# A graph layer's gathers: three of the four groups of a tile are made to wait for TensorE's results

## The chip, the core and the metric

The kernel runs on one core of a Trainium2 chip. Its engines work side by side and wait for each other through semaphores: TensorE (PE, with its weight loads as PEld), VectorE (DVE), ScalarE (ACT), GpSimd (POOL), which here does little more than issue gathers, and SyncE (SP), which issues the plain DMAs. The metric is the time of one execution on the device in microseconds (us).

## The reference, cut to what matters

```python
h = xn @ W                                             # 6250 nodes x 256, 4 heads of 64
e = leaky_relu(a_src[src] + a_dst[dst], 0.2)           # 106250 edges, sorted by dst
ex = exp(e - segment_max(e, dst)[dst])
out = segment_sum(ex * h[src], dst) / segment_sum(ex, dst)
x = x + sigmoid(out + bias) + mix(xn)                  # mix: linear attention with a gate
x = x + ffn(layernorm(x))                              # two layers, 1024 wide; half of the nodes kept
```

The part that matters is `h[src]`: for each edge a row of 260 numbers (256 features and 4 scores) is fetched from memory by the number of its source node.

## The kernel before, in words

Edges are worked through in 52 tiles of 2048 (`NI`, `IE`), nodes in 49 tiles of 128 (`NT`). After a stage that makes the table `feat_d` there is one long block in which every engine runs the same list of parts per step k (`steps`), some parts with a lag: in step k the edges of tile k are scored, weighted and summed, node tile k-5 is merged and gated (`MERGE`), k-6 is summed and normed (`SUM`), k-7 goes through the feed-forward layers (`FF1`, `GELU`), k-8 is put out (`OUT`). Steps 0 to 4 also hold the chunks of the attention's context. Steps 10 to 49 are a loop of two steps per round; the steps around it are written out. Each engine works in the order of its own list; there is no scheduler. The last step with gathers to issue is that of tile 51, and after it some steps run without any.

The order of TensorE in a step is: `turn_scores` (L1503, signals `scores_turned`), `first_ff1` (L1573), `turn_maxima` (L1512, signals `max_turned`), `project` (L1556), `other_ff1` (L1573), `first_sums` and `other_sums` (L1545, each signals `sums_done`), `scores_ahead` (L1487), context chunks, `ff2` (L1524, signals `ff2_done`), `mixer` (L1466, then L1474, which signals `gate_done`), `turn_normed` (L1565, signals `xn2_turned`). "Signals" means that the last matmul of the part adds one to the semaphore.

Those who wait for these signals: VectorE's `outputs` (L1164) for `ff2_done`, `maxima` (L1142, L1145) for `scores_turned`, `differences` (L1154) for `max_turned`; ScalarE's `gates` (L1390, L1394) for `gate_done` and `keep_turned` (L1400) for `xn2_turned`. TensorE's `first_ff1` in turn waits for `keep_turned`. ScalarE's `hidden` (L1407) reads both halves of the first layer, `keep_one` (L1379) copies the sums out, and VectorE's L1134 ends the leaky scores that `turn_scores` turns. L1171 is the product of rows and weights, whose four parts the sums wait for.

GpSimd's `fill(k)` issues 16 gathers for tile k in 4 groups of 4 (`GI`, `TG`), each gather 128 rows, into one of two halves of `ring`. A group may be written when the sums of tile k-2 have read the half: groups 0 and 1 wait for its first sums, groups 2 and 3 for its other ones. VectorE's `scores(k)` needs all four groups, about a step after they are asked for.

Of the kernel before, what the change touches and what calls it, by code (L numbers as in the profile page):

```python
# [42 lines left out]
LAG_MERGE, LAG_SUM, LAG_FF1, LAG_OUT = 5, 6, 7, 8  # L43
# [20 lines left out]
def known_below(i, n):  # L64

    return isinstance(i, int) and i < n


def number(eng, v):

    return v if isinstance(v, int) else eng.snap(eng.to_reg(v))


def gps_layer(nc, x, src, dst, W, att_src, att_dst, gnn_bias, Wqkv, Wproj, bproj, ln_g, ln_b, Wg1, bg1, Wg2, bg2,
# [16 lines left out]
    with ExitStack() as ctx:  # L91
# [5 lines left out]
        def S(name):  # L97

            if name not in named:
                named[name] = ctx.enter_context(nc.semaphore(name))  # L100
            return named[name]
# [121 lines left out]
        with nc.Block() as block:  # L223
# [29 lines left out]
            @block.sync  # L253
            def _(sp):
                sp.dma_start(ed_i[:, 0:IE], src.rearrange("(k e) -> k e", e=IE)).then_inc(S("edges_in"), 16)
                sp.dma_start(ed_i[:, IE:2 * IE], dst.rearrange("(k e) -> k e", e=IE)).then_inc(S("edges_in"), 16)
                for o, i in wide:
                    sp.dma_start(o, i).then_inc(S("weights_in"), 16)
                with nc.allow_non_contiguous_dma(reason="small columns"):
                    for o, i in columns:  # L260
                        sp.dma_start(o, i).then_inc(S("weights_in"), 16)
                for n in range(7):
                    sp.dma_start(big[:, n * XC:(n + 1) * XC, :],
                                 x.rearrange("(t p) c -> p t c", p=P)[:, n * XC:(n + 1) * XC, :]).then_inc(S(f"x{n}_in"), 16)
                for o, i in later:
                    sp.dma_start(o, i).then_inc(S("ffn_in"), 16)

                sp.wait_ge(S("breaks_made"), 1)
                for h in range(HEADS):
                    sp.dma_start(brk_d[:, :, h, :], br_f.rearrange("k (g e) -> k g e", g=GI)).then_inc(S("lists_out"), 16)  # L270
                sp.wait_ge(S("dloc_made"), 2)
                sp.dma_start(dloc_d, dl_b).then_inc(S("lists_out"), 16)
                sp.wait_ge(S("zeroed"), 1)
                sp.dma_start(adst_d[NT * P:ROWS, :], zero[:, 0:SPLIT // 2].bitcast(BF16)).then_inc(S("zeros_out"), 16)
                sp.wait_ge(S("ffn_in"), 32)
# [372 lines left out]
        def gather(pool, u, g):  # L648

            for j in range(TG):  # L650
                q = g * TG + j
                pool.indirect_dma_start(  # L652
                    out=ring[:, u * TI + q, 0:AW], out_offset=None, in_=feat_d,
                    in_offset=bass.IndirectOffsetOnAxis(ap=idx[:, u, q:q + 1], axis=0),
                ).then_inc(S(f"rows_in{u}{g}"), 16)
# [182 lines left out]
        def steps(eng, parts_of_body):  # L838

            loop_from = LAG_OUT + 2 + (LAG_OUT % 2)

            def body(k, u):
                for lo, hi, f in parts_of_body:
                    if lo <= (k if isinstance(k, int) else loop_from) < hi:
                        f(k - lo, (u - lo) % 2)
            for k in range(loop_from):
                body(k, k % 2)
            loop_to = NI - 2 - NI % 2  # L850
            with eng.Fori(loop_from // 2, loop_to // 2) as half:
                for u in range(2):
                    body(half * 2 + u, u)
            for k in range(loop_to, NT + LAG_FF1):
                body(k, k % 2)
# [39 lines left out]
        with nc.Block() as block:  # L895
            @block.gpsimd
            def _(pool):
                def fill(k, u):
                    for g in range(GI):
                        made, used = number(pool, k + 1), None  # L900
                        if not known_below(k, 2):
                            used = number(pool, NB * (k - 2) + g // 2 + 1)
                        pool.wait_ge(S("idx_made"), 2)
                        if g == 0:
                            pool.wait_ge(S("idx_made"), made)
                        if used is not None:
                            pool.wait_ge(S("sums_done"), used)
                        gather(pool, u, g)

                steps(pool, [EDGES(fill)])  # L910
                pool.wait_ge(S("scores_done"), NI)
                pool.iota(hotT[:, 0:30].bitcast(I32), pattern=[[1, 15]], base=1, channel_multiplier=0
                          ).then_inc(S("digits_made"), 1)
# [742 lines left out]
```

## Time and profile before

| | |
|---|---|
| Time, median of 3 runs | 2197.3 us (2191.99 to 2205.76) |
| Profiled execution | 2191.5 us, its span 2189.4 us |
| Mean granted TensorE clock | 0.721 |
| Busy: PE, PEld, DVE, ACT, POOL | 53%, 42%, 49%, 26%, 38% |
| Moved by DMA | 210.63 MB, mean 96 GB/s |

No engine is busy for much more than half of the span. The page's chain of the last work covers only the end of the program, since it breaks off at the first wait whose end it can't name, so it says nothing on the middle, where the time is.

### The profile page before, as it was taken

Reading aid. Unit: us, or ns where it says so; the run is one execution under the profiler, and the core shown is the slowest. Engines: PE = TensorE matmul, PEld = TensorE weight load, DVE = VectorE, ACT = ScalarE, POOL = GpSimd, SP = SyncE. Lnnn points to the kernel's source line nnn. Section 1 sums busy time; section 2 is a strip of 40 time slices with the busy share of each in tenths; the row PEclk is TensorE's granted clock in tenths of the full one; section 3 lists DMA queues with packets and bytes.
Section 4 is the critical chain, followed back from the end, with each engine's and each line's share of the span. In section 5 each row is a group of like instructions: output and inputs, shape, how many; then the busy total and the mean of one; then the engine's idle time right before and its main releaser. Section 6 shows DMA issues by size and latency. Waiting matters only on the chain. (4 is left out here: it accounts for less than half of the span.)

```text
span 2189.4 us, 27080 instructions
## 1 busy us (share of the span) xinstructions
PE 1152.6 (53%) x6567; PEld 909.7 (42%) x6567; DVE 1077.7 (49%) x2779; ACT 564.1 (26%) x1347; POOL 827.8 (38%) x872
## 2 busy tenths in 40 slices
PE   1993455445555555454545454545454545454682
PEld 1772233334444344444444444444444444343571
DVE  8883354544444444444444444444444444353557
ACT  2442122122222222222222222222222222232360
POOL 3003435255353534343434343434343434343200
PEclk9997566767676767676767676767676767676795
DMA  8556334243232323232333233333332333333203
GB/s 238 175 189 118 103 92 125 72 114 98 75 98 75 96 76 92 80 92 80 92 80 94 78 93 79 92 80 92 80 93 79 94 78 90 82 90 82 71 22 117
DMA packets 165932, 210.63 MB, mean 96 GB/s; under 512 B 51115, under 2 KB 130539, under 8 KB 165791
## 3 DMA queue, kind: packets, MB, share of 16 engines
q0 software_dynamic: 39936, 110.81, 19.8%
q1 hardware_dynamic: 125959, 99.41, 16.1%
q8 instruction: 14, 0.23, 0.0%
q14 instruction: 23, 0.19, 0.0%
HBM read 165.80 MB, written 44.30 MB: 96 GB/s over the span
## 5 line engine op out<-in xcount | busy, mean ns | idle before, releaser
L652 POOL DMA_INDIRECT ring<-feat_d,idx x832 | 802.4, 964 | 1066.2 <-issue 556.0
L1573 PE MATMUL bank<-late,w_s 128*128 128x128 f32 x1568 | 311.3, 381 | 678.9 <-ACT late L1400 676.0
L1573 PEld LDWEIGHTS bank<-late,w_s 128*128 128x128 f32 x1568 | 303.0, 292 | 702.4 <-issue 643.3
L1164 DVE TENSOR_TENSOR big<-bank,b2row 128x256 f32 (+1 forms) x49 | 20.8, 424 | 621.3 <-remote 621.3
L1390 ACT ACTIVATE sc<-bank,hbg 128x128 f32<-128x128 f32 x98 | 30.7, 364 | 820.9 <-remote 809.7
L1171 DVE TENSOR_TENSOR ring<-ring,bank 128x1024 f32<-128x1024 f32 x208 | 240.0, 1217 | 1.8 <-ACT bank L1360 1.8
L1545 PE MATMUL bank<-ring,hot 128*64 128x265 f32 x1664 | 212.3, 407 | 38.9 <-DVE ring L1171 32.5
L1524 PE MATMUL bank<-w_s,hT 128*128 128x256 f32 x784 | 185.9, 390 | 3.7 <-ACT hT L1407 3.7
L1545 PEld LDWEIGHTS bank<-ring,hot 128*64 128x64 f32 x1664 | 121.7, 143 | 113.1 <-issue 50.8
L1524 PEld LDWEIGHTS bank<-w_s,hT 128*128 128x128 f32 x784 | 146.9, 193 | 22.7 <-ACT hT L1407 4.3
L1407 ACT ACTIVATE hT<-bank,b_s 128x128 f32<-128x128 f32 x392 | 110.6, 372 | 42.3 <-PE bank L1573 41.7
L1423 PE MATMUL bank<-big,sc 128*128 (+1 forms) x196 | 69.5, 501 | 89.3 <-ACT big L1341 53.9
L1423 PEld LDWEIGHTS bank<-big,sc 128*128 128x128 f32 x196 | 43.3, 242 | 112.2 <-issue 84.4
L1360 ACT ACTIVATE bank<-diff 128x64 f32<-128x64 f32 x52 | 11.8, 228 | 295.8 <-DVE diff L1158 283.2
L1556 PE MATMUL bank<-wproj_s,sc 128*128 128x256 f32 x196 | 86.2, 585 | 0.0
L1379 ACT ACTIVATE wout<-bank 128x265 f32<-128x265 f32 x104 | 40.9, 393 | 162.2 <-PE bank L1545 162.2
L1503 PE MATMUL bank<-ident,lk 128*16 128x128 f32 x208 | 35.3, 292 | 85.8 <-issue 61.8
L1142 DVE TENSOR_TENSOR_SCAN forth<-brk,bank 16x512 f32<-16x512 f32 x52 | 62.5, 1202 | 22.5 <-remote 14.6
L1032 DVE TENSOR_TENSOR late<-late,big 128x256 f32<-128x256 f32 x49 | 20.9, 426 | 103.7 <-ACT big L1341 53.7
L1089 DVE TENSOR_TENSOR hot<-bank,dlocT 128x512 f32<-128x512 f32 x104 | 66.5, 680 | 0.0
L1154 DVE TENSOR_TENSOR ring<-bank,lastT 128x64 f32<-128x64 f32 x52 | 11.7, 225 | 110.7 <-PE bank L1512 105.3
L1407 ACT ACT_TABLE_LOAD x49 | 62.9, 1283 | 8.7 <-PE bank L1573 7.9
(231 smaller groups left out, 1733.8 us busy)
## 6 DMA issues: line engine op xcount, KB each, us to landing
parts_d<-wout SPq DMA_DIRECT2D x208, 66.2 KB
lists<-dloc_d SPq DMA_DIRECT2D x104, 128.0 KB
ring<-feat_d,idx POOLq DMA_INDIRECT x832
parts_d<-hot SPq DMA_DIRECT2D x50, 265.0 KB, 2.9
parts<-parts_d SPq DMA_DIRECT2D x49, 265.0 KB
xs<-in_x SPq DMA_DIRECT2D x74, 128.0 KB
feat_d<-parts SPq DMA_DIRECT2D x49, 130.0 KB, 2.8
big<-in_x SPq DMA_DIRECT2D x7, 896.0 KB, 11.1
```

The lines of the kernel that those rows point to most:

```text
L652: pool.indirect_dma_start(out=ring[:, u * TI + q, 0:AW], out_offset=None, in_=feat_d, in_offset=bass.IndirectOffsetOnAxis(ap=idx[:, u, q:q ...
L1089: V.tensor_tensor(hot[:, tiles, :], iota_ps.unsqueeze(1).to_broadcast([P, 2 * TG, WIN]), dlocT[:, bass.ds(k, 1), tiles].rearrange("p a q - ...
L1142: V.tensor_tensor_scan(forth[:, :], brk[:, 0:GE], bk_t[0:TI, :], LOWEST, ALU.add, ALU.max).then_inc(S("forth_made"), 1)
L1171: V.tensor_tensor(feats, feats, ex[:, g * TG:(g + 1) * TG, :].unsqueeze(3) .to_broadcast([P, TG, HEADS, HD]), ALU.mult).then_inc(S("scaled ...
L1379: A.activation(wout[:, n, :], bank[2 + n][:, 0:SW], ACT.Copy).then_inc(S("sums_kept"), 1)
L1407: A.activation(hT[:, m, :], bank[6 + m // 4][:, (m % 4) * P:(m % 4 + 1) * P], ACT.Gelu_apprx_tanh, bias=b1_s[:, m:m + 1]).then_inc(S("gelu ...
L1423: mm = T.matmul(bk_c[t][:, 0:C], sc[:, u, t * P:(t + 1) * P], big[:, bass.ds(i, 1), :].rearrange("p a c -> p (a c)"), start=s, stop=e)
L1503: mm = T.transpose(bk_t[0:TI, :].rearrange("r (e j) -> r j e", j=TG)[:, j, :], lk[:, u, j, :], ident[:, :])
L1524: mm = T.matmul(bk_o[:, 0:C], hT[:, m, :], w2_s[:, m, :], start=(m == 0), stop=(m == FT - 1))
L1545: mm = T.matmul(bank[2 + n][c * WIN:(c + 1) * WIN, 0:SW], hot[:, q, :], ring[:, u * TI + q, 0:SW], start=(j == 0), stop=(j == TG - 1))
L1556: mm = T.matmul(bk_t[:, 0:C], sc[:, u, t * P:(t + 1) * P], wproj_s[:, t, :], start=(t == 0), stop=(t == CT - 1))
L1573: mm = T.matmul(bank[6 + m // 4][:, (m % 4) * P:(m % 4 + 1) * P], w1_s[:, t, m * P:(m + 1) * P], xn2T[:, t * P:(t + 1) * P], start=(t == 0 ...
```

## The change

Per tile k and group g of the gathers one more wait is put ahead of the group's first gather. Group 1 waits for `ff2_done` of step k-2, group 2 for `scores_turned` of step k-1, group 3 for `max_turned` of step k-1. Group 0 is as before. The waits are left out where there is nothing yet to wait for (group 1 up to tile 8, groups 2 and 3 of tile 0). No instruction moves on TensorE, VectorE, ScalarE or SyncE.

```diff
-                        made, used = number(pool, k + 1), None
+                        made, used, pace = number(pool, k + 1), None, None
                         if not known_below(k, 2):
                             used = number(pool, NB * (k - 2) + g // 2 + 1)
+                        if g == 1 and not known_below(k, LAG_FF1 + 2):
+                            pace = ("ff2_done", number(pool, k - LAG_FF1 - 1))
+                        if g >= 2 and not known_below(k, 1):
+                            pace = (("scores_turned", "max_turned")[g - 2], number(pool, k))
                         pool.wait_ge(S("idx_made"), 2)
                         if g == 0:
                             pool.wait_ge(S("idx_made"), made)
+                        if pace is not None:
+                            pool.wait_ge(S(pace[0]), pace[1])
                         if used is not None:
                             pool.wait_ge(S("sums_done"), used)
                         gather(pool, u, g)
```

GpSimd in the loop, the first of its two steps before: two rows are a group of four gathers, and L71 makes a number for a wait.

```order
150 L652 DMA ring<-feat_d,idx 128x260 [waits sums_done,idx_made]
151 L652 DMA ring<-feat_d,idx 128x260 x3
152 L652 DMA ring<-feat_d,idx 128x260 [waits sums_done,idx_made]
153 L652 DMA ring<-feat_d,idx 128x260 x3
154 L71 ISA
155 L652 DMA ring<-feat_d,idx 128x260 [waits sums_done,idx_made]
156 L652 DMA ring<-feat_d,idx 128x260 x3
157 L652 DMA ring<-feat_d,idx 128x260 [waits sums_done,idx_made]
158 L652 DMA ring<-feat_d,idx 128x260 x3
```

And the same step now:

```order
150 L652 DMA ring<-feat_d,idx 128x260 [waits sums_done,idx_made]
151 L652 DMA ring<-feat_d,idx 128x260 x3
152 L71 ISA
153 L652 DMA ring<-feat_d,idx 128x260 [waits sums_done,ff2_done,idx_made]
154 L652 DMA ring<-feat_d,idx 128x260 x3
155 L71 ISA
156 L652 DMA ring<-feat_d,idx 128x260 [waits sums_done,scores_turned,idx_made]
157 L652 DMA ring<-feat_d,idx 128x260 x3
158 L71 ISA
159 L652 DMA ring<-feat_d,idx 128x260 [waits sums_done,max_turned,idx_made]
160 L652 DMA ring<-feat_d,idx 128x260 x3
```

The gathers stand in the same order; three of the four groups have one more name in their waits, and two more numbers are made for them.

## Rows read from the trace of the kernel before

**Rows 1.** The page: busy by engine, and the costliest groups' idle time and releasers.

```profile
PE 1152.6 (53%) x6567; PEld 909.7 (42%) x6567; DVE 1077.7 (49%) x2779; ACT 564.1 (26%) x1347; POOL 827.8 (38%) x872
...
L1573 PE MATMUL bank<-late,w_s 128*128 128x128 f32 x1568 | 311.3, 381 | 678.9 <-ACT late L1400 676.0
```

**Rows 2.** Waits from 530 to 2055 us: who waited for whom, sum, times, longest.

```profile
ACT sc L1390 <- remote: 786.9, 42, 19.2
PE bank L1573 <- ACT late L1400: 657.1, 42, 16.3
...
DVE big L1164 <- remote: 608.7, 42, 15.6
```

**Rows 3.** Timeline of one loop step: start, duration, engine, line, [idle before <- releaser].

```profile
1221.58 2.01 PE L1545 MATMUL bank<-ring,hot 128*64 128x265 f32 x16 [0.66 <-DVE ring L1171]
...
1224.61 1.19 POOL L652 DMA_INDIRECT ring<-feat_d,idx  x1 [15.34 <-PE bank L1545]
...
1226.01 3.70 PE L1524 MATMUL bank<-w_s,hT 128*128 128x256 f32 x16
1226.04 0.39 ACT L1379 ACTIVATE wout<-bank 128x265 f32<-128x265 f32 x1 [1.87 <-PE bank L1545]
...
1228.70 0.94 POOL L652 DMA_INDIRECT ring<-feat_d,idx  x1 [0.31 <-issue]
...
1230.53 0.71 PE L1474 MATMUL bank<-hidT,wg_s 64*128 64x128 f32 x4
...
1233.45 0.60 PE L1503 MATMUL bank<-ident,lk 128*16 128x128 f32 x4 [1.85 <-issue]
...
1243.74 0.95 POOL L652 DMA_INDIRECT ring<-feat_d,idx  x1 [0.30 <-issue]
1247.92 0.42 DVE L1164 TENSOR_TENSOR big<-bank,b2row 128x256 f32 x1 [14.60 <-remote]
1247.95 0.63 ACT L1390 ACTIVATE sc<-bank,hbg 128x128 f32<-128x128 f32 x2 [18.39 <-remote]
...
1253.00 0.66 PE L1512 MATMUL bank<-ident,srow 16*128 16x16 f32 x4
...
1261.55 0.94 POOL L652 DMA_INDIRECT ring<-feat_d,idx  x1 [16.86 <-issue]
```

**Rows 4.** Groups by line on GpSimd, 525 to 2052 us: 42 tiles of 16.

```profile
L652 POOL DMA_INDIRECT ring<-feat_d,idx x672 | 647.2, 963 | 889.5 <-issue 500.3 <-PE bank L1545 389.2
```

**Rows 5.** Timeline: first gathers of the first and the last of these tiles.

```profile
530.75 0.95 POOL L652 DMA_INDIRECT ring<-feat_d,idx  x1 [17.16 <-PE bank L1545]
...
2030.14 1.19 POOL L652 DMA_INDIRECT ring<-feat_d,idx  x1 [15.38 <-PE bank L1545]
```

**Rows 6.** Timeline of a step without gathers.

```profile
2066.19 0.39 ACT L1379 ACTIVATE wout<-bank 128x265 f32<-128x265 f32 x1 [0.81 <-PE bank L1545]
...
2073.35 0.63 ACT L1390 ACTIVATE sc<-bank,hbg 128x128 f32<-128x128 f32 x2 [1.85 <-PE bank L1474]
...
2074.73 0.42 DVE L1164 TENSOR_TENSOR big<-bank,b2row 128x256 f32<-128x256 f32 x1
...
2084.45 0.39 ACT L1379 ACTIVATE wout<-bank 128x265 f32<-128x265 f32 x1 [0.92 <-PE bank L1545]
```

**Rows 7.** Windows: a run of gathers, the 3 us after it, the rest, a step without.

```profile
1225.00:1245.00 20.00, 7.20 (x50) 5.49 (x46) 6.82 (x24) 3.46 (x5) 15.12 (x16) 0.73 0.49 129
1245.00:1248.00 3.00, 0.00 (x0) 0.00 (x0) 0.08 (x1) 0.05 (x1) 0.00 (x0) 0.50 0.19 45
1248.00:1261.50 13.50, 12.21 (x68) 10.43 (x70) 10.51 (x19) 5.73 (x17) 0.00 (x0) 0.63 0.11 32
2066.00:2084.00 18.00, 15.13 (x115) 12.48 (x112) 14.93 (x38) 9.13 (x22) 0.16 (x1) 1.00 0.16 40
```

**Rows 8.** Timeline, context stage: a run of gathers begins at 254.8 us.

```profile
258.71 0.94 POOL L652 DMA_INDIRECT ring<-feat_d,idx  x1 [0.30 <-issue]
...
263.36 0.60 ACT L1349 ACTIVATE sc<-xs,rstd_neg,rstd 128x256 f32<-128x256 f32 x1 [3.40 <-remote]
...
273.84 0.94 POOL L652 DMA_INDIRECT ring<-feat_d,idx  x1 [0.30 <-issue]
...
277.47 0.60 ACT L1349 ACTIVATE sc<-sa,rstd_neg,rstd 128x256 f32<-128x256 f32 x1 [3.33 <-PE bank L1423]
```

## The prediction

> **What bounds the kernel now.** I read the page's busy shares first, then the waits of the looped stretch, then the timeline of one step, and last a step without gathers. The busy shares show no engine above 53% [rows 1], so the time is in waits. The waits show which: 42 times ScalarE's gates wait for a release that the profile can't place ("remote"), 18.7 us each, 42 times VectorE's L1164 does, 14.5 us each, and TensorE's first layer waits behind ScalarE for 15.6 us each [rows 2].
>
> The timeline shows what it is. Call T the start of a tile's first gather (1224.61). TensorE ends ff2 at 1229.71 (T+5.1), the gate at 1231.24 and the turned scores at 1234.05 (T+9.4). Yet VectorE, which asked for ff2_done, starts at 1247.92 and ScalarE, which asked for gate_done, at 1247.95: two engines, two semaphores, both from TensorE, one moment. What lies between is GpSimd's run of 16 gathers, whose last record ends at 1244.69; both are released 3.2 us later [rows 3]. In the step without gathers the same two waits don't exist: the gate ends and ScalarE starts, VectorE doesn't idle at L1164, and the step takes 2084.45 - 2066.19 = 18.3 us [rows 6]. So I read: **while gathers are under way, TensorE's signals are held back and delivered together about 3.2 us after the last gather's record.** Not all are held: the other sums' signal, given 1.2 us after T, reached ScalarE at once (1226.04); ff2_done, given as the fourth gather ended, did not [rows 3]. I take it that a signal passes in roughly the first three or four gathers of a run and is held after. The delay after a run is 2.7 us at the shortest (274.78 to 277.47) and 3.7 us at the longest (259.65 to 263.36, where the run went on) [rows 8].
>
> A step lasts (2030.14 - 530.75)/41 = 36.57 us [rows 5]: run of gathers 20.1, delay 3.2, then 13.3 in which the turned scores become maxima and weights and the first sums free the ring. The middle 3 us have no compute at all [rows 7]. The step's end is set by "run + delay + 13.3", and the run is long because nothing interrupts it.
>
> A rule speaks against this reading. The Trainium skill, "SBUF — State Buffer", section "SBUF: two separate sides", says that DMA and compute engines use disjoint ports and can't slow each other. The held signals aren't data in SBUF, so rows and rule need not collide, but by the rule as it stands the gathers would be innocent; that case is among the rivals.
>
> **The change part by part.**
>
> *Added instructions.* Three waits and two made numbers a tile, on GpSimd, which idles 889.5 us in this stretch [rows 4]: nothing. The numbers are made while it would wait anyway. Behind each wait are queued that group's gathers and all later ones of GpSimd, nothing else. Nobody needs the rows early: VectorE reads tile k's scores some 8 us after the next T (leaky scores end just before 1233.45 = T+8.8), and all of tile k's groups must be issued before GpSimd can start the next tile. If the last group ended just at the next T, its rows would still have those 8 us against the 3.2 us delay. No transfer is added, and no other queue moves.
>
> *The run is cut.* What counts is how many pieces it falls into, since between pieces the held signals come through. One gap costs the delay 3.2 plus GpSimd's start after a signal: first sums end at 1223.59, first gather 1224.61, 1.0 us [rows 3]; 4.2 us together. I follow the step with the durations of the old one:
> - Group 0 runs T to T+5.0. ff2_done (T+5.1) is held, as before; it comes at T+8.2. First gap. With it come the gate and xn2_turned, so ScalarE and VectorE restart at T+8.2 and not at T+23.3.
> - Group 1 starts at T+9.2. The scores are turned at T+9.4, in its first gather: the signal passes, so group 2 follows without a gap, to T+18.9.
> - From the release to the end of L1512 took 1253.66 - 1247.92 = 5.7 us, most of it the first layer at the lower granted clock (0.50, that is 1.2 GHz) after an idle TensorE [rows 3, 7]. Counted from the scores, max_turned comes at about T+13.9, 4.7 us into the run of groups 1 and 2: held, until T+22.1. Second gap; group 3 from T+23.1 to T+27.8.
> - From max_turned to the first sums' end it takes 6.9 us now at the lower clock (the next run starts at 1261.55, so they end at 1260.55, less 1253.66) [rows 3] and less if TensorE is busier; say T+28 to T+29. That falls late in group 3 or behind it: held until T+31.0. Third gap; next T at T+32.
> Where ff2_done comes early enough to pass, groups 0 and 1 join and the scores are held instead: again three pieces. So I count **three gaps a step**: 16 records of 0.95, 13 spacings of 0.30 within pieces, 3 x 4.2 = 15.2 + 3.9 + 12.6 = 31.7 us. Against 36.57 that is 4.87 less, in 42 steps 204 us. The compute (18.3 us when nothing holds it) lies under it, with its waits beside the pieces.
>
> *The first tiles.* Context tiles in steps 0 to 4 wait 3.4 us each for TensorE under gathers [rows 8]; groups 2 and 3 now move out from beside them into the next step, where they can hold the first sums. Bounds: nothing, and 30 us gained (two such waits less in each of four or five steps). I take 10 gained.
>
> *Sum.* 2191.5 - 204 - 10 = 1977.5 on the profiled execution, which lay some 6 us below the median of the runs shown; I say **1980 us**. With the delay at 2.7 or 3.7 a step is 30.2 or 33.2 us and the time 1914 or 2040: this case's own range.
>
> A second figure: the Trainium skill, "DMA: Bandwidth & Descriptors", section "Anatomy of one DMA — SWDGE (gpsimd) path", gives some 2.0 us as fixed cost of such a DMA. The rows' 3.2 us behind a run is more than that. With 2.0 for the delay, as an estimate, three gaps would be 9.0 us, a step 28.1 and the time near 1826.
>
> **The rivals.**
> - *Two gaps.* max_turned misses the cut by about a us. At the full clock the first layer is quicker, and if it passes, three groups join: 15.2 + 14 x 0.30 + 8.4 = 27.8 us, 8.77 less, 368 over 42 steps: **1813 us**. For it: less idle time keeps the clock higher (1.00 in the step without gathers, 0.50 in the hold [rows 7]). Against: each gap still leaves TensorE idle just ahead of this layer. With the short delay 1771.
> - *Four gaps.* Every signal is held by the group before it, GpSimd and TensorE hand the step to and fro: 15.2 + 3.6 + 16.8 = 35.6 us, 41 less: **2140 us**, with the 10 at the start. Against: the turned scores come too close behind the first release.
> - *Four long gaps, slower.* Place: the same four waits. Price: with the longest delay, 3.7 + 1.0 = 4.7, a step is 18.8 + 18.8 = 37.6, 1.0 more, 43 in all: **2235 us**. It decides from a gap of (36.57 - 18.8)/4 = 4.44 us. For it: the chain of waits now runs through GpSimd four times, and SyncE's DMAs, which lay behind the run, now fall into gaps and could lengthen them.
> - *The gathers are innocent.* Something else ends these waits, and it keeps its period; the gathers wait to no purpose, still off the path: **2191 us**. This is what the rule on separate ports would give. Against it stand two engines released together 3.2 us after the run in step after step, and no such wait without gathers [rows 2, 3, 6].
>
> **How the numbers follow.** Three gaps 0.43; two gaps, or shorter ones, 0.32; four gaps 0.10; innocent 0.06; slower 0.09. About 1% (22 us) is what a measurement of this kernel can tell from no change. Faster by over 1%: 0.43 + 0.32 + most of the four gaps = 0.83; within 1%: 0.08; slower 0.09. The range leaves out the slower case, the innocent one, and a little of the fast end: 1790 to 2145.
>
> **What the profile after would show.** Right: GpSimd's gathers in pieces of 4 and 8 with pauses of 4 us; the waits at L1164 and L1390 down from 14.5 and 18.7 us to under 8; a period near 32 us; a higher mean clock. Two gaps: pieces of 12 and 4 or 8 and 8, period near 28. Wrong: signals held although only four gathers are under way and for longer than 3.7 us; or L1164 waiting 14 us beside an idle GpSimd, which would clear the gathers. What would spoil the sum most is a hold that begins with the first gather of a piece, or SyncE's issues beside a piece that hold TensorE's signals by themselves.

## The result and the profile after

| | before | after |
|---|---|---|
| Time, median | 2197.62 us (2191.99 to 2205.76, 4 runs) | 1728.38 us (1719.49 to 1730.59, 4 runs) |
| Profiled execution, its span | 2191.5, 2189.4 us | 1730.59, 1728.5 us |
| Mean granted TensorE clock | 0.721 | 0.833 |

The ratio is 0.7855, 95% interval 0.7818 to 0.7892. The change saved 469 us, where the prediction had 217, and the time lies below the range of 1790 to 2145. Line numbers after are 6 higher (L1154 is now L1160, L1164 is L1170, L1390 is L1396, L1573 is L1579, L1545 is L1551, L1512 is L1518).

The page after, with the busy shares and three of the costliest groups, answers to [rows 1]:

```profile
PE 1125.7 (65%) x6567; PEld 860.7 (50%) x6567; DVE 1076.8 (62%) x2779; ACT 559.1 (32%) x1347; POOL 838.2 (48%) x872
...
L1551 PE MATMUL bank<-ring,hot 128*64 128x265 f32 x1664 | 311.3, 529 | 279.0 <-DVE ring L1177 147.2
...
L1579 PE MATMUL bank<-late,w_s 128*128 128x128 f32 x1568 | 218.3, 299 | 14.0 <-ACT late L1406 12.2
...
L1160 DVE TENSOR_TENSOR ring<-bank,lastT 128x64 f32<-128x64 f32 x52 | 11.7, 225 | 248.9 <-remote 231.1
```

The work is the same, and so are VectorE's and ScalarE's busy times. TensorE's idle time ahead of the first layer went from 678.9 to 14.0 us. The layer's matmuls also went from 381 to 299 ns each, with a mean granted clock of 0.833 instead of 0.721. What is left is idle time ahead of the sums, and their matmuls, which now follow on it, went from 407 to 529 ns (in the step below at a granted clock of 0.69, in the one of [rows 3] at 1.00).

The waits after, over 491 to 1600 us, answer to [rows 2]: engine, line, releaser, sum, times, longest.

```profile
DVE ring L1160 <- remote: 217.9, 38, 7.9
...
PE bank L1551 <- DVE ring L1177: 131.2, 21, 7.6
...
ACT hT L1413 <- remote: 99.5, 21, 7.8
...
ACT sc L1396 <- PE bank L1480: 70.8, 39, 2.8
```

The gates (L1396) now begin when TensorE's gate ends, in 39 of 41 steps. The waits that the profile calls "remote" moved to L1160, which asks for `max_turned`, and they are 5.7 us each instead of 14.5 to 18.7.

The timeline of one step after answers to [rows 3]: start, duration, engine, line, idle time before and its releaser.

```profile
1259.96 0.95 POOL L652 DMA_INDIRECT ring<-feat_d,idx  x1 [2.24 <-PE bank L1551]
...
1260.88 3.70 PE L1530 MATMUL bank<-w_s,hT 128*128 128x256 f32 x16
...
1263.92 0.95 POOL L652 DMA_INDIRECT ring<-feat_d,idx  x1 [0.30 <-issue]
...
1266.15 0.62 ACT L1396 ACTIVATE sc<-bank,hbg 128x128 f32<-128x128 f32 x2 [1.71 <-PE bank L1480]
...
1266.93 0.94 POOL L652 DMA_INDIRECT ring<-feat_d,idx  x1 [2.06 <-issue]
...
1268.43 0.87 PE L1509 MATMUL bank<-ident,lk 128*16 128x128 f32 x4 [1.95 <-DVE lk L1140]
...
1272.38 0.65 PE L1518 MATMUL bank<-ident,srow 16*128 16x16 f32 x4
...
1275.68 0.94 POOL L652 DMA_INDIRECT ring<-feat_d,idx  x1 [0.30 <-issue]
...
1278.81 0.22 DVE L1160 TENSOR_TENSOR ring<-bank,lastT 128x64 f32<-128x64 f32 x1 [6.87 <-remote]
...
1279.65 0.94 POOL L652 DMA_INDIRECT ring<-feat_d,idx  x1 [3.03 <-issue]
...
1283.40 0.95 POOL L652 DMA_INDIRECT ring<-feat_d,idx  x1 [0.30 <-issue]
...
1286.16 0.39 ACT L1385 ACTIVATE wout<-bank 128x265 f32<-128x265 f32 x1 [2.58 <-PE bank L1551]
...
1286.98 0.95 POOL L652 DMA_INDIRECT ring<-feat_d,idx  x1 [2.63 <-issue]
```

GpSimd's run of 16 is in three pieces in this step. Group 0 ends at 1264.87; `ff2_done` (TensorE ended ff2 at 1264.58) reaches GpSimd so that group 1 starts at 1266.93, after a gap of 2.06 us. The turned scores (L1509, end 1269.30) pass while group 1 is under way, so groups 1 and 2 are one piece of eight, to 1276.62. `max_turned` (L1518 ends at 1273.03) is held: VectorE gets it at 1278.81, 2.2 us after the piece, and group 3 starts after a gap of 3.03 us. The third gap, 2.63 us, is no hold at all: the first sums end 1.6 us behind the last piece, ScalarE starts on them at 1286.16, and GpSimd 0.8 us after it.

Not every step is like this one. Of the 41 from tile 10 to tile 51, 24 have the gap ahead of group 3. In the 17 others GpSimd finds `max_turned` there already: in three the signal passed within 0.3 us, and in 14 it was late but came in the midst of the piece of eight, as here:

```profile
1326.13 0.65 PE L1518 MATMUL bank<-ident,srow 16*128 16x16 f32 x4
...
1329.27 0.95 POOL L652 DMA_INDIRECT ring<-feat_d,idx  x1 [0.30 <-issue]
1330.16 0.22 DVE L1160 TENSOR_TENSOR ring<-bank,lastT 128x64 f32<-128x64 f32 x1 [4.45 <-remote]
...
1330.52 0.95 POOL L652 DMA_INDIRECT ring<-feat_d,idx  x1 [0.30 <-issue]
```

The signal is given at 1326.78 and VectorE gets it 3.4 us later with gathers on both sides. So a signal is late beside gathers, but it need not wait for the end of their run. Steps with the gap ahead of group 3 last 27.0 us in the mean, those without it 25.8.

The window of the first of these steps answers to [rows 7]: busy times of PE, PEld, DVE, ACT and POOL, granted clock, DMA share, GB/s.

```profile
1260.00:1287.00 27.00, 18.64 (x118) 14.76 (x116) 16.96 (x43) 9.12 (x22) 15.31 (x17) 0.81 0.44 116
```

Where the time went: the first gather of tile 10 starts at 491.71 (530.75 before, [rows 5]) and that of tile 51 at 1578.8, so a step is 1087.1/41 = 26.51 us instead of 36.57. That is 412 us in 41 steps; 39 us lie ahead of tile 10 and 10 us behind the start of tile 51; together 461, the difference of the spans.

### The profile page after: what moved, and what is told of

It is laid out like the page before. It is cut to its first block and busy times, and to the rows that moved or that the text cites. A ratio compares the mean times of both kernels' runs of the same rounds, so it can differ in the third digit from the quotient of the medians.

```text
span 1728.5 us, 27082 instructions
## 1 busy us (share of the span) xinstructions
PE 1125.7 (65%) x6567; PEld 860.7 (50%) x6567; DVE 1076.8 (62%) x2779; ACT 559.1 (32%) x1347; POOL 838.2 (48%) x872
## 3 DMA queue, kind: packets, MB, share of 16 engines
q0 software_dynamic: 39936, 110.81, 25.5%
## 5 line engine op out<-in xcount | busy, mean ns | idle before, releaser
L652 POOL DMA_INDIRECT ring<-feat_d,idx x832 | 812.7, 977 | 606.1 <-issue 501.8
L1551 PE MATMUL bank<-ring,hot 128*64 128x265 f32 x1664 | 311.3, 529 | 279.0 <-DVE ring L1177 147.2
L1551 PEld LDWEIGHTS bank<-ring,hot 128*64 128x64 f32 x1664 | 175.2, 188 | 398.8 <-issue 324.0
L1579 PE MATMUL bank<-late,w_s 128*128 128x128 f32 x1568 | 218.3, 299 | 14.0 <-ACT late L1406 12.2
L1579 PEld LDWEIGHTS bank<-late,w_s 128*128 128x128 f32 x1568 | 211.8, 214 | 19.3 <-ACT late L1406 8.3
L1160 DVE TENSOR_TENSOR ring<-bank,lastT 128x64 f32<-128x64 f32 x52 | 11.7, 225 | 248.9 <-remote 231.1
L1212 DVE TENSOR_SCALAR late<-sd,bn 128x256 f32<-128x256 f32 x49 | 21.5, 438 | 130.0 <-issue 69.6
L1509 PE MATMUL bank<-ident,lk 128*16 128x128 f32 x208 | 33.7, 288 | 81.7 <-DVE lk L1140 65.7
L1518 PE MATMUL bank<-ident,srow 16*128 16x16 f32 x208 | 32.8, 269 | 50.9 <-issue 27.5
L1151 DVE TENSOR_TENSOR_SCAN srow<-brk,forth 16x512 f32<-16x512 f32 x52 | 63.0, 1212 | 1.8
```

Source lines behind the costliest of these rows:

```text
L652: pool.indirect_dma_start(out=ring[:, u * TI + q, 0:AW], out_offset=None, in_=feat_d, in_offset=bass.IndirectOffsetOnAxis(ap=idx[:, u, q:q ...
L1151: V.tensor_tensor_scan(srow[:, :][:, ::-1], brk[:, 1:GE + 1][:, ::-1], forth[:, :][:, ::-1], LOWEST, ALU.add, ALU.max).then_inc(S("max_mad ...
L1509: mm = T.transpose(bk_t[0:TI, :].rearrange("r (e j) -> r j e", j=TG)[:, j, :], lk[:, u, j, :], ident[:, :])
L1551: mm = T.matmul(bank[2 + n][c * WIN:(c + 1) * WIN, 0:SW], hot[:, q, :], ring[:, u * TI + q, 0:SW], start=(j == 0), stop=(j == TG - 1))
L1579: mm = T.matmul(bank[6 + m // 4][:, (m % 4) * P:(m % 4 + 1) * P], w1_s[:, t, m * P:(m + 1) * P], xn2T[:, t * P:(t + 1) * P], start=(t == 0 ...
```

## The experiments

Each run has the kernel before beside it on the same chip. The runs below fell on five chips; runs with the same figure for before share one (the chip of the first measurement isn't known). A "step" is (first gather of tile 51 less first gather of tile 10)/41 in that run's trace, and "first" is the start of tile 10's first gather. Runs without an interval are single ones.

| run | time | before beside it | first | step |
|---|---|---|---|---|
| changed kernel | 1728.4 | 2197.6 | 491.7 | 26.51 |
| only_g1 | 1868.1 | 2199.9 | 533.0 | 28.86 |
| only_g2 | 1711.9 | 2199.9 | 484.8 | 26.27 |
| only_g3 | 1921.1 | 2199.9 | 506.1 | 30.75 |
| pause2 | 1668.5 | 2199.9 | 455.9 | 26.01 |
| pause1 | 1880.1 | 2195.3 | 471.9 | 30.71 |
| pause15 | 1712.9 | 2195.3 | 457.9 | 26.80 |
| pausemid | 1934.9 | 2195.3 | 475.5 | 31.76 |
| narrow | 2198.8 | 2195.3 | 537.9 | 36.61 |
| twice | 1750.3 | 2236.7 | 468.8 | 27.59 |
| threes | 1775.2 | 2236.7 | 463.3 | 28.45 |
| pairs | 1907.6 | 2236.7 | 474.9 | 31.19 |
| direct | 1349.6 | 2236.7 | 411.4 | 19.36 |
| pause2b | 1624.5 | **1404.3** | 446.0 | 25.25 |
| pause18 | 1597.8 | **1404.3** | 439.1 | 24.71 |
| mix | 1528.8 | **1404.3** | 429.2 | 23.21 |
| rows64 | 1383.3 | **1404.3** | 420.5 | 20.04 |
| after2 | 1721.2 | 2188.0 | 490.3 | 26.50 |
| rows64b | 2211.7 | 2188.0 | 574.5 | 35.99 |

**One wait at a time.** The changed kernel with one of its three waits and the two others removed:

```diff
-                        if g == 1 and not known_below(k, LAG_FF1 + 2):
-                            pace = ("ff2_done", number(pool, k - LAG_FF1 - 1))
-                        if g >= 2 and not known_below(k, 1):
+                        if g == 2 and not known_below(k, 1):
```

This is the edit for the scores' wait alone; the two others are alike.

> Only group 1 waits (for ff2_done); groups 2 and 3 as before. Theory of runs (TensorE's signals are held from about the fourth gather of a run on, and come 1.1 us after the end of a run of 4, 2.1 after 8, 3.1 after 16): pieces 4 and 12, the scores still pass, max_turned is held until about T+24.6, a step of about 31 us, so about 1930 us. Rival, that the gain belongs to one of the three waits because of what its group then runs beside: either the whole gain (1730 us) or none (2190 us) in one of the three kernels with a single wait.

> Only group 2 waits (for scores_turned). Theory of runs: pieces 8 and 8; the scores are released 2.1 us after the first piece, max_turned comes 5.2 us later and is held by the second: a step of about 31 us, about 1930 us; should max_turned pass, 25.5 us and 1690 us. Rival: the whole gain or none.

> Only group 3 waits (for max_turned). Theory of runs: pieces 12 and 4; all is released 2.6 us after the first, max_turned follows 5.7 us later, the first sums 5.5 after that: a step of about 31 us, about 1920 us. Rival: the whole gain or none.

Measured: 1868.1, 1711.9 and 1921.1 us. The maxima's wait came out as expected, and the scores' wait near the second of its two figures (1690). The wait for `ff2_done` took 62 us less than the 1930 expected, since `max_turned` wasn't held to the end of the piece of twelve: in 26 of 41 steps it came in the midst of it. The timeline with only the wait for the turned scores (group 2):

```profile
782.27 0.71 PE L1478 MATMUL bank<-hidT,wg_s 64*128 64x128 f32 x4
...
786.47 0.95 POOL L652 DMA_INDIRECT ring<-feat_d,idx  x1 [0.30 <-issue]
...
789.40 0.63 ACT L1394 ACTIVATE sc<-bank,hbg 128x128 f32<-128x128 f32 x2 [8.04 <-remote]
...
790.43 0.95 POOL L652 DMA_INDIRECT ring<-feat_d,idx  x1 [3.02 <-issue]
...
794.45 0.66 PE L1516 MATMUL bank<-ident,srow 16*128 16x16 f32 x4
...
795.24 0.22 DVE L1158 TENSOR_TENSOR ring<-bank,lastT 128x64 f32<-128x64 f32 x1 [2.40 <-issue]
```

Two pieces of eight with a gap of 3.0 us. The maxima's turning ends at 795.11, between the third and the fourth gather of the second piece, and passes at once, as in 40 of 41 steps. One well-placed wait gives what the three give together, a step of 26.3 us; the two others buy nothing beyond it. The wait for `ff2_done` begins only with tile 9 and alone brings no early gain (tile 10 starts at 533.0), so the 39 us ahead of tile 10 come from groups 2 and 3. With only the maxima's wait a piece has twelve gathers:

```profile
1197.24 0.94 POOL L652 DMA_INDIRECT ring<-feat_d,idx  x1 [0.30 <-issue]
...
1200.83 0.42 DVE L1168 TENSOR_TENSOR big<-bank,b2row 128x256 f32 x1 [10.16 <-remote]
1200.91 0.62 ACT L1394 ACTIVATE sc<-bank,hbg 128x128 f32<-128x128 f32 x2 [13.69 <-remote]
```

The signals come 2.65 us after its last record (1198.18). So, where a signal is held to the end of its piece, the lateness behind it is in the steps shown 1.1 us for four (a gap of 2.06 less the 1.0 us of GpSimd's start), 2.2 for eight, 2.65 for twelve, 3.2 for sixteen [rows 3]. It grows with the piece. Over all 41 steps the gates' signal was 2.0 us late behind eight (median of 39, 1.8 to 2.3, with the scores' wait alone), 2.7 behind twelve (2.4 to 2.9) and 3.35 behind sixteen (3.05 to 3.65, in the kernel before).

**Pauses instead of waits.** Rival: the gathers are innocent, and the waits only line the engines up. The kernel before, with no wait for TensorE, and GpSimd filling an unused buffer ahead of groups 1 to 3:

```diff
+        idle = sb("idle", [P, 2048])
...
+                        for at in idled:
+                            pool.wait_ge(S("pool_made"), at)
+                            pool.memset(idle[:, :], 0.0).then_inc(S("pool_made"), 1)
                         gather(pool, u, g)
```

> The kernel before with no new wait for TensorE: GpSimd fills a buffer of its own with 2048 zeros per partition ahead of groups 1, 2 and 3, about 2 us each, whatever the other engines do. Theory of runs: a pause of 2 us lets a run of 4 end (1.1 us) and the held signals through, GpSimd itself sets the step at 4 x 4.7 + 3 x 2.5 us, about 26.5 us, so about 1730 us, as with the waits. Rival, that what counts is where in TensorE's step each group lies: pauses that know nothing of it leave most of the old step, over 2000 us; and if the gathers are innocent of the hold, each pause only lengthens GpSimd's work and the step stays at 36.6 us, 2190 us.

Measured: 1668.5 us. GpSimd does more than before, it waits for no more signals than before, and 531 us are gone. The gaps alone do it, and the rival falls. The timeline:

```profile
1209.91 0.71 PE L1479 MATMUL bank<-hidT,wg_s 64*128 64x128 f32 x4
...
1212.43 0.95 POOL L653 DMA_INDIRECT ring<-feat_d,idx  x1 [0.30 <-issue]
1213.38 1.82 POOL L912 MEMSET idle<- 128x2048 f32 x1
...
1213.59 1.64 DVE L1130 COPY idx<-srcT 128x16 int32 x1
...
1215.37 1.00 POOL L653 DMA_INDIRECT ring<-feat_d,idx  x1 [0.17 <-POOL idle L912]
1215.54 0.42 DVE L1169 TENSOR_TENSOR big<-bank,b2row 128x256 f32 x1
...
1217.54 0.63 ACT L1395 ACTIVATE sc<-bank,hbg 128x128 f32<-128x128 f32 x2 [8.55 <-remote]
```

A gap is 1.99 us. The gate's result gets through only 2.2 us into the next piece: even 2.0 us don't let everything through. (VectorE's L1169 was not kept waiting here; it came to it late. The fill has a price of its own: the copy L1130, with a median of 0.165 us, took 1.64 us beside it, and L1211, which takes some 0.47 us apart from the fills, took 2.2 us in the mean in the 15 cases beside one. VectorE's products of rows and weights stayed at 1.22 us. So a longer pause also costs VectorE more.)

**How long must a gap be?** The same with fills of 1024 and 1536 columns (970 and 1397 ns), and with a single fill of 2048 ahead of group 2.

> The kernel before with an idle fill of 1024 columns ahead of GpSimd's second, third and fourth group of gathers, half of the 2048 of the run before, and no wait for TensorE. The fill of 2048 columns took 1.82 us and left 2.0 us between pieces, so this one leaves about 1.15 us, which is just the 1.1 us that a signal of TensorE was late after a piece of four gathers in the changed kernel. If the stillness needed is that 1.1 us, the signals still come through in most gaps: the step loses three times 0.9 us against the 26.0 of the wide fill, some 23.5 us, and the time is near 1565. If the stillness needed is longer, the pieces count as one run of 16 and the step goes back to about 36.6 plus the pauses' 3 us, so 2190 to 2300.

> The same with a fill of 1536 columns: about 1.37 us, a gap of 1.6 us. With a stillness of 1.1 us needed after four gathers the step is 26.0 minus three times 0.45, 24.7 us, and the time 1668 minus 42 times 1.3, some 1612. If 1.6 us are too short it is 2190 or more, as with the narrowest fill.

> The kernel before with one idle fill of 2048 columns, ahead of the third group alone: two pieces of eight gathers with 2.0 us between them. After a piece of eight TensorE's signals were 2.1 us late in the changed kernel. If the lateness after a piece is stillness that the signals need, 2.0 us is a little short and the signals of the first half mostly stay held: a step of about 36.6, 2190. If a gap of 2.0 us is enough whatever the piece's length, it is the run with the wait on the turned scores alone (26.27 us a step) less 1 us of gap, 25.3 us and 1670.

Measured: 1880.1, 1712.9 and 1934.9 us. I had neither threshold right: 1.13 us after four gathers and 2.0 after eight lose many signals, but not all, and 1.57 let more through than 1.13 but fewer than 2.0. The gates' waits of this kind over 530 to 1500 us, in the waits of before, with gaps of 1.13, and with gaps of 2.0:

```profile
ACT sc L1390 <- remote: 487.4, 26, 19.1
```

```profile
ACT sc L1395 <- remote: 368.9, 31, 19.5
```

```profile
ACT sc L1395 <- remote: 109.3, 13, 13.7
```

With gaps of 1.57 it is 207.2 us in 20 times, with one gap of 2.0 in the middle 332.1 in 30. A gap just as long as the lateness measured behind a piece is at the edge; of the gaps tried behind four gathers the longest, 2.0 us, did best.

**Finer and fewer pauses.** Fills inside a group, behind the gathers named:

```diff
+                if q in (5, 10):
+                    pool.wait_ge(S("idx_made"), 2)
+                    pool.wait_ge(S("pool_made"), at.pop(0))
+                    pool.memset(idle[:, :], 0.0).then_inc(S("pool_made"), 1)
```

(3, 6, 9, 12) with 1024 columns is `threes`, (2, 4, ... 14) with 512 is `pairs`.

> The kernel before with two idle fills of 2048 columns a tile, behind the 5th and the 10th gather: pieces of 5, 5 and 6 with 2.0 us between them. If a gap must only be longer than the piece's own lateness (1.1 us after four, 2.1 after eight, so some 1.3 to 1.6 after five and six), signals come through twice inside the run and GpSimd sets the step: 20.0 us of gathers, two times 1.7 us more, and 1.2 us from the first sums to the next tile's first gather, 24.6 us; 1668 minus 42 times 1.4, about 1610. If the step needs a release every five microseconds it comes out slower than the three fills' 1668 in spite of the shorter run.

> The kernel before with four idle fills of 1024 columns a tile, behind every third gather: pieces of 3, 3, 3, 3 and 4 with 1.15 us between them. With pieces of four such gaps were at the edge (1880). If lateness grows with the piece from nothing, pieces of three need under 1.1 us, the signals come through each time, and the step is 20.0 plus four times 0.85 plus 1.2, 24.6 us: about 1610. If 1.15 us are at the edge whatever the piece's length, the time stays near 1880 or above.

> The kernel before with seven idle fills of 512 columns a tile, behind every second gather: pieces of two with about 0.65 us between them. If what counts is a gap against the length of its piece (a backlog that each gather adds to and each still stretch drains), 0.65 us after two gathers is as good as 1.3 after four, and the step is 20.0 plus seven times 0.35 plus 1.2, 23.7 us: about 1570, or up to 1750 if the drain is just short. If a gap must be over some fixed 1 us to let signals through, the run counts as whole and the time is 2190 to 2290.

Measured: 1750.3, 1775.2 and 1907.6 us, each 140 to 340 above the expectation that had the signals come through every time. The total still time between pieces (4.0, 4.5 and some 5 us a tile) isn't what counts: `pairs` have the most of the three and do worst. `threes` with 1.13 us gaps did better than `pause1` with the same gaps (1880), so shorter pieces need shorter gaps. What puts the seven kernels with pauses in order is the gap against the number of gathers ahead of it, with the time against the kernel before beside each:

| run | gap, us, behind gathers | gap per gather | time / before |
|---|---|---|---|
| pausemid | 1.98 behind 8 | 0.25 | 0.881 |
| pause1 | 1.13 behind 4 | 0.28 | 0.856 |
| pairs | 0.70 behind 2 | 0.35 | 0.853 |
| threes | 1.13 behind 3 | 0.38 | 0.794 |
| pause15 | 1.56 behind 4 | 0.39 | 0.780 |
| twice | 1.99 behind 5 | 0.40 | 0.783 |
| pause2 | 1.99 behind 4 | 0.50 | 0.758 |

These are single runs on three chips, so the 0.003 between two of them says nothing; the order as a whole is what `pairs` expected of a backlog that each gather adds to and each gap drains. That there is such a backlog is not shown.

**What about the gathers holds the signals?** First, bytes: 80 instead of 1040 per row, most of each feature row left out.

```diff
-                    out=ring[:, u * TI + q, 0:AW], out_offset=None, in_=feat_d,
+                    out=ring[:, u * TI + q, 0:20], out_offset=None, in_=feat_d.rearrange("r (a c) -> (r a) c", a=13),
```

> The kernel before, without pauses or waits, whose gathers fetch 20 columns of a row (80 bytes) where they fetched 260 (1040 bytes); the ring is filled with zeros once, and the rows read are others, so most of each feature row is left out. As many gathers, and as many rows in each. If TensorE's signals are held by the bytes that the gathers move, the hold shrinks to a thirteenth, the step falls to GpSimd's 20.1 us and a little, and the time to 1500 to 1600. If they are held by the gathers' instructions and descriptors as such, the step stays 36.6 us and the time near 2190.

Measured: 2198.8 us beside 2195.3. Its timeline:

```profile
1252.27 0.95 POOL L652 DMA_INDIRECT ring<-feat_d,idx  x1 [0.30 <-issue]
...
1256.75 0.42 DVE L1165 TENSOR_TENSOR big<-bank,b2row 128x256 f32 x1 [14.93 <-remote]
1256.79 0.63 ACT L1391 ACTIVATE sc<-bank,hbg 128x128 f32<-128x128 f32 x2 [18.80 <-remote]
```

3.5 us after the last record; over 41 steps the gates' signal was 3.4 us late (3.0 to 3.7), as with 13 times the bytes (3.35). The bytes don't matter. Second, rows: gathers of the first 64 partitions alone (`out=ring[0:64, ...]`, `idx[0:64, ...]`), so half of the neighbours are left out.

> The kernel before, without pauses or waits, whose gathers fetch only the rows of the first 64 partitions; the other half of the ring stays zero, so half of the neighbours are left out. As many gather instructions, half as many rows in each. If the hold goes by descriptors against time (a backlog), it is gone or shorter: with gathers that still take 0.95 us the signals are prompt and the step is GpSimd's 20.1 plus 1.2 us or less, 1450 to 1500. If it goes by the gather instructions alone, step and time stay as they are, 36.6 and 2190. If the instruction shortens with its rows to about half, the run is 10 us: then 10 plus 3 plus 13.3, 26.4 us and 1765, with the hold, and some 19 us and 1350 to 1450 without.

> Again the kernel before with gathers that fetch only the rows of the first 64 partitions (half of the neighbours are left out), which took 1383 on the chip where before took 1404, and so told nothing of the hold. Its gathers took 0.945 us each, as those of 128 rows do. On a chip that holds signals back: near 2190 with steps of 36.6 us if the hold goes by gather instructions; 1400 to 1500 if it goes by the rows or descriptors of a gather. On one that doesn't: 1383 again.

The first of these fell on the chip that is told of below. The second took 2211.7 us beside 2188.0, and its timeline shows the hold whole:

```profile
1241.27 0.90 POOL L652 DMA_INDIRECT ring<-feat_d,idx  x1 [0.30 <-issue]
...
1246.23 0.42 DVE L1165 TENSOR_TENSOR big<-bank,b2row 128x256 f32 x1 [14.40 <-remote]
1246.28 0.62 ACT L1391 ACTIVATE sc<-bank,hbg 128x128 f32<-128x128 f32 x2 [18.67 <-remote]
```

Half the rows, and 4.1 us after the last record here and in the median of 41 steps (3.8 to 4.3): if anything later. It goes by gather instructions, neither by bytes nor by rows. Third, the kind of transfer: plain copies of 128 neighbouring rows, also started by GpSimd (the sums are then of other rows).

```diff
-                pool.indirect_dma_start(
-                    out=ring[:, u * TI + q, 0:AW], out_offset=None, in_=feat_d,
-                    in_offset=bass.IndirectOffsetOnAxis(ap=idx[:, u, q:q + 1], axis=0),
-                ).then_inc(S(f"rows_in{u}{g}"), 16)
+                pool.dma_start(ring[:, u * TI + q, 0:AW], feat_d[q * P:(q + 1) * P, :]).then_inc(S(f"rows_in{u}{g}"), 16)
```

> The kernel before, without pauses or waits, in which each of GpSimd's gathers is a plain copy of 128 rows that stand together (the q-th block of the table), started by GpSimd: as many transfers of the same shape and bytes into the same places, but without an index; the sums are of other rows. If TensorE's signals are held by the writing of descriptors for gathers with an index alone, the hold goes and the step falls to the other engines' 18.3 us or to GpSimd's run, whichever is longer: 1350 to 1650. If they are held by any transfer that GpSimd starts, the hold lasts as long as the sixteen take, and the step is their run plus 3 plus 13 us, as before.

Measured: 1349.6 us beside 2236.7. A run of 16 takes 8.6 us instead of 20.1, and inside it TensorE's signals arrive at once:

```profile
817.78 8.62 POOL L652 DMA_DIRECT2D ring<-feat_d  x16 [10.34 <-PE bank L1542]
...
823.91 0.71 PE L1471 MATMUL bank<-hidT,wg_s 64*128 64x128 f32 x4
...
824.66 0.62 ACT L1387 ACTIVATE sc<-bank,hbg 128x128 f32<-128x128 f32 x2 [1.72 <-PE bank L1471]
```

The gate ends at 824.62, ScalarE starts at 824.66, 6.9 us into the run. Same bytes and packets (39936), same shape, same queue: only the gather with an index holds TensorE's signals. In all 41 steps the gate's signal came through at once, in the twelfth or thirteenth copy. The window of that step shows what the engines can do without the hold, at the full clock:

```profile
817.80:837.30 19.50, 15.66 (x118) 12.45 (x116) 16.71 (x42) 9.12 (x22) 8.48 (x17) 1.00 0.55 161
```

**A chip that doesn't hold.** Three more kernels: `pause2` again, the same with fills of 1792 columns, and `mix`, with fills of 1792 ahead of groups 1 and 3 and the scores' wait ahead of group 2.

> The kernel before with idle fills of 2048 columns ahead of the second, third and fourth group of gathers, timed in rounds: 1668 once, so 1660 to 1680 again, 3 to 4 per cent under the changed kernel's 1728 and some 24 per cent under the kernel before.

> The same with fills of 1792 columns, 1.6 us each and gaps of 1.77 us. One fill of 1536 gave 1713 (signals missed in every second step or so), 2048 gave 1668 (none missed). If 1.77 us still let every signal through, the step loses three times 0.22 us: 25.3 us and 1640. If some are missed it lies between the two, 1670 to 1700.

> Fills of 1792 columns ahead of the second and fourth group, and ahead of the third the wait for the turned scores, which of the three waits cost least alone. After a piece of four the lateness is 1.1 us and GpSimd starts 1.0 us after the signal, so the third gap is 2.1 us where the scores were turned in time. Step 25.5 us, time 1650 to 1665, and steps that a missed gap would lengthen are held back by the wait. If the wait comes later than the gap (scores that are not yet turned), the step is 26.3 us as with that wait alone, 1680 to 1710.

(`pause18` starts from "none missed" with 2048 columns. That isn't so: the 13 waits of the gates above are of `pause2`.) The three fell on a chip on which the kernel before took 1404.25 us (1397.62 to 1409.55, 7 runs) and not 2188 to 2237 as on the four others. Ratios there: 1.1575 (1.152 to 1.1629), 1.1392 (1.1339 to 1.1446), 1.0905 (1.0852 to 1.0958). The timeline of `mix`, inside a piece of eight gathers:

```profile
911.20 0.96 POOL L653 DMA_INDIRECT ring<-feat_d,idx  x1 [0.16 <-POOL idle L915]
...
913.71 0.95 POOL L653 DMA_INDIRECT ring<-feat_d,idx  x1 [0.30 <-issue]
...
914.11 0.71 PE L1482 MATMUL bank<-hidT,wg_s 64*128 64x128 f32 x4
...
914.86 0.62 ACT L1398 ACTIVATE sc<-bank,hbg 128x128 f32<-128x128 f32 x2 [1.72 <-PE bank L1482]
...
914.96 0.95 POOL L653 DMA_INDIRECT ring<-feat_d,idx  x1 [0.30 <-issue]
```

The gate ends at 914.82 and ScalarE starts 0.04 us later, with gathers on both sides. The gathers last the same 0.95 us, but nothing is held. `rows64`, also run there, shows a step of 20.04 us there: GpSimd issues its 16 gathers back to back, tile after tile, and is what bounds the kernel (the kernel before has no trace on this chip, and its 1404 us lie 21 above those of `rows64`). So every pause costs its full length: 25.25, 24.71 and 23.21 us a step for 5.1, 4.4 and 2.9 us that their gaps add (three of 1.99, three of 1.77 and two of 1.77, less 0.30 each). The changed kernel once more:

> The changed kernel once more. On the chip of the last four runs the kernel before took 1404 and TensorE's signals came through at once in the midst of gathers; on the chips of all the runs ahead it took 2195 to 2237. If this run is on a chip that holds signals back, before is near 2200 and the changed kernel near 1728, as first measured. If it is on one that doesn't, before is near 1404, there is nothing for the three waits to win, each still costs the wait for its signal and 1 us of start, and GpSimd's run of 20.1 us grows to some 23 (the mixed form with one such wait and two pauses had steps of 23.2 us and took 1529): 1450 to 1560, slower by 3 to 11 per cent.

It fell on a chip that holds: 1721.18 us (1715.28 to 1729.26) beside 2187.97 (2182.84 to 2196.8, 7 runs), ratio 0.7854 (0.7827 to 0.7882), the first result again. Its steps had the same shape as well: 24 of 41 with a gap ahead of group 3, 17 without. The changed kernel itself was never timed on the chip that doesn't hold, and `mix` doesn't say what its waits would cost there: the one of them that `mix` has never made GpSimd wait (0.30 us ahead of group 2 in all 41 steps), and what `mix` lost it lost to its two fills. Nor do runs on one occasion for each chip tell the chip from the occasion.

## Why the prediction was wrong, point by point

**Right: what bounds.** TensorE's signals are held back by a long run of gathers, and in the kernel before they come behind it (the gates' signal in 41 of 41 steps, `ff2_done` in 39). Pauses without any wait (`pause2`), plain copies (`direct`) and the piece-by-piece timelines show it. This is so on the four chips where before takes about 2200 us, as in the measurement predicted for.

**Right in 24 steps of 41: three gaps a step**, of pieces of 4, 8 and 4, held `ff2_done`, passing scores, held `max_turned`, as the prediction followed it. The third is not what it said: in the step shown the first sums ended 1.6 us behind the last piece and weren't held.

**Wrong: "held, until T+22.1" for every step.** In the 17 other steps `max_turned` was there before the piece of eight ended, in 14 of them after a delay, and the pieces of 8 and 4 joined. [rows 8] had shown such a case: the wait that ends at 263.36 ends with the run still going on, as the prediction says itself, but it counted this as a delay behind a run. It is the smaller part of the miss: with three gaps in every step the mean would be 27.0 us, not 26.51.

**Wrong: "one gap costs the delay 3.2 plus GpSimd's start after a signal; 4.2 us together".** This is the step that failed. The 3.2 us were read behind runs of 16 and put behind pieces of 4 and 8. They measured 1.1 and 2.2 us, and no lateness was left for the third; the gaps were 2.06, 3.03 and 2.63 us in the step shown, 7.7 instead of 12.6. With 15.2 + 3.9 + 7.7 = 26.8 the old sum would have been right within 0.3 us of the 27.0 that such steps take. (31.7 - 26.51) x 42 = 218 us of the 247 that the forecast missed on the profiled execution, some 197 of them by the size of the gaps and 21 by the steps that lack one. The start after a signal, 1.0 us, was right. The own range, 2.7 to 3.7, came from a run of 16 of the context stage (2.7 behind it, 3.7 in its midst) and could not contain a delay that depends on the run's length. `only_g2` (2.0 after eight) and `only_g3` (2.65 after twelve) show the growth apart from the change.

**Wrong in size: the first tiles.** 10 us with a bound of 30; 39 measured, 29 of the miss. The waits of groups 2 and 3 win them (`only_g2` 46, `only_g3` 25, `only_g1` none). That they do it by releasing the context chunks' signals is argued from [rows 8], and not shown; `pause2`, with no wait for TensorE, starts tile 10 earlier still, at 455.9.

**The second figure.** The Trainium skill, "DMA: Bandwidth & Descriptors", section "Anatomy of one DMA — SWDGE (gpsimd) path", with its 2.0 us gave 1826 as an estimate. That was nearer than the forecast, but it is a fixed amount, and the runs show 1.1 to 3.35 us by the length of the piece.

**The rivals.** Two gaps (1813, 1771 with the short delay) is what 17 of the 41 steps did, at 25.8 us and not 27.8, since its gaps too were priced at 4.2; as a figure it came nearer than the forecast, but by luck: too high a price for too few gaps. `only_g2` has two gaps in every step, with pieces of eight, and took 1711.9. Four gaps and the slower case didn't come, since the scores did pass. "The gathers are innocent" falls on the holding chips. It is how the other chip behaves. The rule of the Trainium skill, "SBUF — State Buffer", section "SBUF: two separate sides", that a transfer doesn't slow an engine's own access, decides nothing here. The traces agree with it: VectorE's products of rows and weights took 1217 ns each in the kernel before, where they fall between the runs, and 1217 in `rows64`, where gathers never stop. But a held signal isn't an access, and the page says nothing on it.

**The marks.** Pieces of 4 and 8 (in 24 steps of 41), waits under 8 us at L1170 (none) and L1396 (7.3 at the longest), and a higher clock: as written. Pauses of 4 us and a period near 32: not so.

**What stays open.** What in the chip does the holding, why a held signal comes in the midst of a piece in some steps and behind it in others, and why one chip of five doesn't hold, is not settled: all that is shown is what it goes by (gathers with an index, in number, close together) and what it doesn't (bytes, rows, the queue as such). Whether the changed kernel is slower than before on the chip that doesn't hold was not measured. On the chips that hold, `pause2` took 0.758 of before in a single run, against 0.785 for the change; on the other it took 1.158. No version here is known to be the fastest on every chip.

## What to carry over

When two engines wait for different signals of a third and start at one moment, look for what ends just before that moment on an engine that isn't in the chain, and measure the delay at several lengths of it: a delay read behind one length is no constant. If a long run of one engine holds others back, cut it, and a single cut in the right place may do (the scores' wait alone: 1711.9 us) where three gave nothing more. A cure for what one chip does must be timed on others: the same pauses took 24% off on one chip and added 16% on another. And look at all steps before one is taken for the rule: the one shown here is one of 24, and the 17 others went another way.

## What the runs showed of the hardware

- GpSimd's gathers with an index, 16 in a row at 1.25 us each, held TensorE's signals to VectorE and ScalarE until 3.05 to 3.65 us behind the last record (the gates' signal, given in the fifth or sixth gather, in 41 steps of 41). After 4, 8 and 12 it was 1.1, 2.0 to 2.2 and 2.65 us. 80 bytes a row instead of 1040 (3.4 us) and 64 rows instead of 128 (4.1 us) change nothing for the better.
- A held signal can also come in the midst of a run: `max_turned`, given in the fourth or fifth gather of a piece, did so in 15 of 41 steps of the changed kernel (in one of them only in the last gather) and in 26 of 41 of `only_g1`. Given in the third, it passed at once in 40 of 41 steps of `only_g2`.
- Pauses let the signals through by the gap against the number of gathers ahead of it: from 0.25 us per gather (0.881 of before) to 0.50 (0.758).
- Plain copies of the same shape from the same engine, 0.54 us each, hold nothing (0.04 us from the gate's end to ScalarE's start), and the kernel with them took 1349.6 us.
- GpSimd's fills of 0.55 to 1.8 us let held signals through, the more the longer they are. They slow VectorE in places: its L1211 (a tensor with a scalar) took 2.2 us in the mean beside a fill of 1.82 us and 0.47 apart from them, its copies L1130 1.1 and 0.17, while its products of two tensors, L1176, took 1.22 us either way.
- One chip of five held nothing: 1404 us for the kernel before, 36% less than on the others, and no gate's signal late in any step of the four traces taken there, with gathers just as long (0.95 us).
